# Attention and feed-forward kernel: fillers, one root and two unpacks reordered behind the loop, and six tiles' output base added on GpSimd inside it

## The chip, the cores and the metric

The kernel runs on one core of one Trainium2 chip. The metric is the device time in microseconds of one execution; the median of several runs is compared.

## The reference, cut to what matters

```python
x = x + L0_xattn(layernorm(x), tok, ctx, ctx, ctx)      # gated experts, one of four per token
x = x + L0_ffn(layernorm(x), w8)                        # fp8-quantised product
x = x + L1_xattn(layernorm(x), ctx, Wq, bq, Wkv, bkv, Wp, bp)
x = x + L1_ffn(layernorm(x), weight, bias)
```

x is (4, 256, 256) in f32, 1024 tokens of 256. Of the four steps two matter here:

```python
def L1_xattn(x, cond, ...):                 # 16 heads of 16, 1024 queries, 1024 keys
    q = fq_sym((x @ Wq + bq) * scale); k, v = fq_sym(cond @ Wkv + bkv)
    attn = fq_unsigned(softmax(q @ k.T))    # per head, rounded to 255 steps
    return (attn @ v) @ Wp + bp
def L1_ffn(x, weight, bias):
    return x @ ternary_quantize(weight).T + bias
```

## The kernel before, in words

The 1024 tokens lie in 8 tiles of 128 rows, sorted by expert. Each engine has its own program, written out by hand; semaphores tie them together. The first part (to about 118 us) makes keys, values, queries and the first two steps.

**The attention loop** runs over 8 tiles t and in each over 16 heads u. For one head TensorE makes the scores of 128 queries against 1024 keys (L1284) into one of three score buffers of two PSUM banks; VectorE takes the negative maximum of each row (`nmax`, L969); GpSimd makes the exponent's bias from it (`ebias`, `exp_bias`, L462); ScalarE makes the exponential, rounded to bytes (even heads) or 16-bit integers (odd heads) (L639). TensorE may write the scores of head u + 3 only when the exponential of head u is done. After every pair of heads SP's queue issues a transposing DMA (L362). What lands is in `rawT` (the trace calls its memory `ksplit`). The odd head is used from there; the even head's bytes must be unpacked to 16 bits into `byteT` (the trace says `gates`), by GpSimd in two casts of 128x512 (`unpack`, L473), which are called as the steps of the even and the odd head, 6 heads behind the bias. TensorE weighs the values with them 7 heads behind (`weigh`, L1313). To fill TensorE, `weigh` first issues four transposes that nobody reads (L1306), except where `fillers=False`.

In the same loop work of the tile before is put in: VectorE inverts the sums of the exponentials behind head 1 (L1001), divides behind head 9 (L1013), adds the projection to `xs` behind head 15 (`x3_ready`, L1007). GpSimd adds the projection's bias to `xs` in two halves, behind the casts at heads 9 and 10 (L484).

**Behind the loop** the work of the last tile and all of the fourth step remain. The tiles are in five units: (0, 1), (2, 3), (4, 5), (6), (7). For each unit: sums of the rows (`fourth_sums`, L1035 and L1039, VectorE), inverse root (`fourth_root`, L411 and L412, GpSimd; three roots, for tiles 0-1, 2-6 and 7), norm (`fourth_norm`, L932, VectorE), transposes (`h4_turn`, L1360, TensorE), copy (`copy_h4`, L665, ScalarE), products (`ternary`, L1371, TensorE), `output_base` (x + bias into `x4`, called `vq` in the trace; L1047, VectorE), `add_ternary` (L1052, VectorE), indirect store (`scatter_output`, L499, GpSimd, one per tile). In between the last tile's remaining heads 9 to 15 are weighed (`late_weigh`), divided, transposed (`att_turn`, L1321) and projected (`project`, L1329). Every engine takes its own list in order: GpSimd's is root 0, casts of heads 10 to 13, root 1, casts of 14 and 15, stores of units 0 and 1, root 2, stores of units 2 to 4.

## Time and profile before

| | us |
|---|---|
| three runs | 311.62, 311.80, 314.02 |
| median | 311.8 |
| the profiled execution | 311.21 |
| its span | 309.3 |
| busy in the span: VectorE / TensorE / ScalarE / GpSimd | 255.4 / 215.7 / 203.5 / 175.3 |

The profile is of one execution. Its rows give a start in microseconds from the start of the span, a busy time, the engine (PE is TensorE, PEld its weight load, DVE VectorE, ACT ScalarE, POOL GpSimd, SPq SP's queue), the line of the kernel, what is written from what, and how many instructions are merged into the row (x6). In square brackets stands idle time of the engine ahead of the row, and what ended it. Starts and ends of neighbours on VectorE overlap by some hundredths.

### The profile page before, as it was taken

Reading aid. Unit: us, or ns where it says so; the run is one execution under the profiler, and the core shown is the slowest. Engines: PE = TensorE matmul, PEld = TensorE weight load, DVE = VectorE, ACT = ScalarE, POOL = GpSimd, SP = SyncE. Lnnn points to the kernel's source line nnn. Section 1 sums busy time; section 2 is a strip of 40 time slices with the busy share of each in tenths; the row PEclk is TensorE's granted clock in tenths of the full one; section 3 lists DMA queues with packets and bytes.
Section 4 is the critical chain, followed back from the end, with each engine's and each line's share of the span. In section 5 each row is a group of like instructions: output and inputs, shape, how many; then the busy total and the mean of one; then the engine's idle time right before and its main releaser. Section 6 shows DMA issues by size and latency. Waiting matters only on the chain.

```text
span 309.3 us, 6042 instructions
## 1 busy us (share of the span) xinstructions
PE 215.7 (70%) x2042; PEld 149.0 (48%) x2072; DVE 255.4 (83%) x393; ACT 203.5 (66%) x352; POOL 175.3 (57%) x354
## 2 busy tenths in 40 slices
PE   4893189756526865587777787877877787776890
PEld 3441057544313751055555555555555555555670
DVE  2560969988869498979999999999999999999550
ACT  1100022544485736799999999999999999995020
POOL 2270242638742101377777767777777777786744
PEclk9999557999756795779999999999999999999787
DMA  7935000005999909979989899899989899899011
GB/s 248 305 110 153 1 1 2 0 0 95 178 197 178 170 0 180 177 146 168 149 172 165 161 155 155 155 159 147 175 160 158 162 169 150 160 155 156 17 52 68
DMA packets 133806, 41.03 MB, mean 133 GB/s; under 512 B 126352, under 2 KB 132880, under 8 KB 133776
## 3 DMA queue, kind: packets, MB, share of 16 engines
q1 hardware_dynamic: 131680, 37.24, 68.2%
q0 software_dynamic: 768, 2.10, 1.9%
q10 hardware_dynamic: 1328, 1.32, 1.3%
q8 instruction: 16, 0.26, 0.4%
q14 instruction: 14, 0.11, 0.1%
HBM read 5.25 MB, written 2.10 MB: 24 GB/s over the span
## 4 chain that ended last, share of the span: by engine, by line
ACT 24%; POOL 21%; DVE 18%; issue 16%; PE 12%; DMA 8%; POOLq 0%; ACTq 0%; DVEq 0%
ACT ctxT L639 11%; ACT ctx L639 11%; POOL gates L473 11%; POOL ebias L462 4%; DMA ksplit<-in_x 3%; PE ps L1155 3%; POOL scratch L406 2%; DMA xs<-scratch 2%; DMA ksplit<-ctxT 2%; POOL rstd L412 2%; DVE nmax L969 2%; PE ps L1284 1%; PE ps L1266 1%; POOL out L499 1%; DVE xs L862 1%
## 5 line engine op out<-in xcount | busy, mean ns | idle before, releaser
L969 DVE TENSOR_REDUCE nmax<-ps 128x1 f32<-128x1024 f32 x128 | 152.4, 1218 | 5.7 <-PE ps L1284 4.2
L1284 PE MATMUL ps<-keysT,kv 128*128 128x512 bf16 x226 | 74.3, 403 | 38.8 <-ACT ctx L639 22.3
L473 POOL CAST gates<-ksplit 128x512 int16<-128x512 uint8 x128 | 78.9, 618 | 10.2 <-DMA ksplit<-ctx 2.5
L639 ACT ACTIVATE ctx<-ps,ebias,qscale 128x1024 uint8<-128x1024 f32 x64 | 76.7, 1202 | 4.4 <-POOL ebias L462 4.4
L639 ACT ACTIVATE ctxT<-ps,ebias,qscale 128x1024 uint8<-128x1024 f32 x64 | 76.5, 1200 | 1.2 <-POOL ebias L462 1.2
L462 POOL TENSOR_SCALAR ebias<-nmax,qscale 128x1 f32<-128x1 f32 x128 | 33.9, 265 | 41.3 <-DVE nmax L969 38.0
L1306 PEld LDWEIGHTS ps<-identb 128*128 128x128 bf16 x400 | 30.9, 99 | 24.7 <-POOL gates L473 1.5
L1306 PE MATMUL ps<-identb 128*128 128x128 bf16 x400 | 39.2, 221 | 0.9 <-POOL gates L473 0.9
L1284 PEld LDWEIGHTS ps<-keysT,kv 128*128 128x128 bf16 x256 | 15.0, 98 | 49.5 <-ACT ctx L639 25.4
L532 ACT COPY hT<-ps 128x256 f32<-128x256 f32 x11 | 4.1, 371 | 46.0 <-PE ps L1147 46.0
L1313 PE MATMUL ps<-vals,gates 128*128 128x16 f16 x512 | 22.4, 170 | 0.4 <-POOL gates L473 0.4
L1313 PE MATMUL ps<-vals,ksplit 128*128 128x16 f16 x512 | 22.3, 170 | 0.1
L1313 PEld LDWEIGHTS ps<-vals,gates 128*128 128x128 f16 x512 | 20.4, 97 | 2.1 <-POOL gates L473 0.6
L1313 PEld LDWEIGHTS ps<-vals,ksplit 128*128 128x128 f16 x512 | 19.8, 96 | 1.2 <-ACT ctxT L639 0.2
L411 POOL TENSOR_SCALAR vareps<-mv 128x1 f32<-128x1 f32 (+4 forms) x14 | 3.7, 261 | 25.3 <-DVE mv L942 12.1
L1155 PE MATMUL ps<-ctxT,hT 128*128 (+1 forms) x44 | 14.8, 469 | 1.6 <-ACT hT L532 1.6
L406 POOL DMA_INDIRECT scratch<-ksplit,dest x8 | 8.5, 1056 | 11.9 <-DMA ksplit<-in_x 9.8
L1130 PE MATMUL ps<-wkv_s,ctxT 128*128 128x512 f32 x32 | 14.4, 598 | 0.7 <-ACT ctxT L526 0.7
L1155 PE MATMUL ps<-ctxT,gates 128*128 (+1 forms) x44 | 13.7, 441 | 0.3 <-ACT gates L538 0.3
L639 ACT ACTIVATION_READ_ACCUMULATOR ctxT<-ps,ebias,qscale 128x1 f32 x64 | 12.6, 196 | 0.0
L639 ACT ACTIVATION_READ_ACCUMULATOR ctx<-ps,ebias,qscale 128x1 f32 x64 | 12.4, 194 | 0.0
L1155 PEld LDWEIGHTS ps<-ctxT,hT 128*128 128x128 f32 x44 | 9.8, 236 | 4.4 <-issue 2.8
(187 smaller groups left out, 336.3 us busy)
## 6 DMA issues: line engine op xcount, KB each, us to landing
keysT<-zeros SPq DMA_DIRECT2D x4, 512.0 KB, 8.2
ctx<-in_ctx SPq DMA_DIRECT2D x2, 512.0 KB, 4.8
ksplit<-in_x ACTq DMA_DIRECT2D x1, 1024.0 KB, 10.8
xs<-scratch SPq DMA_DIRECT2D x1, 1024.0 KB, 5.6
wkv_s<-in_L_xattn_Wkv SPq DMA_DIRECT2D x1, 512.0 KB, 8.0
ksplit<-ctx SPq DMA_TRANSPOSE x32, 3.7
ksplit<-ctxT SPq DMA_TRANSPOSE x32, 3.8
bkv_b<-in_L_xattn_bkv ACTq DMA_DIRECT2D x1, 256.0 KB, 11.3
```

The lines of the kernel that those rows point to most:

```text
L406: g.indirect_dma_start(scratch, bass.IndirectOffsetOnAxis(ap=dest[:, t:t + 1], axis=0), record[:, t, :], None).then_inc(scattered, 16)
L412: root = g.tensor_tensor(rstd[:, lo:hi], vareps[:, lo:hi], half[:, 0:hi - lo], ALU.pow)
L462: g.tensor_scalar(ebias[:, slot], nmax[:, slot], qscale[:, t, u:u + 1], LN255, ALU.mult, ALU.add).then_inc(bias_ready, 1)
L473: g.tensor_copy(byteT[:, w % PT, part, :, :], rawT[:, w % PAIRS, part, :].bitcast(U8).rearrange("p b (q j) -> p b j q", j=2)).then_inc(unp ...
L532: a.copy(hT[:, j % 2, 0:C, :], ps[:, TRB[0], 0:D].rearrange("p (c q) -> p c q", c=C)).then_inc(hT_ready, 1)
L639: a.activation(probs, s_in, ACT.Exp, bias=ebias[:, u % 4:u % 4 + 1], scale=qscale[:, t, u:u + 1], accum_out=lsum[:, t, u:u + 1]).then_inc( ...
L969: v.tensor_reduce(nmax[:, u % 4:u % 4 + 1], score_banks(k, u), AX.X, ALU.max, negate=True).then_inc(max_ready, 1)
L1130: last = m.matmul(ps[:, KVB[r % 4], :], ctxT[:, c, r * P:(r + 1) * P], wkv_s[:, c, :], start=(c == 0), stop=(c == C - 1))
L1155: last = m.matmul(ps[:, bank, 0:D], lhs[:, c, :], ctxT_e[:, c, e, :], start=(c == 0), stop=(c == C - 1))
L1284: last = m.matmul(ps[:, bank + b, :], qT[:, t, u // 2, :], keysT[:, u % 2, u // 2, 512 * b:512 * b + 512], start=True, stop=True)
L1306: m.transpose(idle[:, i * P:(i + 1) * P], identb[:, :], identb[:, :])
L1313: last = m.matmul(out, probT.bitcast(F16), vals[:, r, u * HD:(u + 1) * HD], start=(r == 0), stop=(r == KT - 1))
```

## The change

- Loop, GpSimd: behind the casts at heads 4 and 5, from tile 2 on, half of tile t - 2 is added to the output bias into `x4`, after a wait for that tile's finished `xs` (`x3_ready`). That makes 12 additions of 128x128, for tiles 0 to 5.
- Behind the loop, VectorE: `output_base` 0, 1 and 2 go; a wait for the 12 additions (`based`) takes their place. Norm 3 moves ahead of addition 1, `output_base(3)` behind it, `output_base(4)` ahead of norm 4.
- GpSimd: root 1 moves ahead of the casts of heads 12 and 13 (the list is now root 0, casts 10 and 11, root 1, casts 12 and 13). The casts of heads 14 and 15 go.
- ScalarE: one copy of the same pair's 1024 columns (`unpack_last`), between the copies of turn 0 and turn 1; `weigh` of head 14 waits for it.
- TensorE: `late_weigh` issues its four unread transposes; `keep_warm` issues 10 more behind the loop, 4 behind turn 0 and 8 behind ternary 3; ternary 3 moves ahead of turn 4.

```diff
--- before.py
+++ after.py
@@ -49,6 +49,8 @@
 COPY_AT = 10
 PROJECT_AT = 11
 ADD_AT = 15
+BASE_AT = 4
+BASES = 6
 UNITS = ((0, 1), (2, 3), (4, 5), (6,), (7,))
 ROOTS = ((0, 2), (2, 7), (7, 8))
 
@@ -266,6 +268,7 @@
         linv_ready, att_ready, x3b_ready = sem("linv_ready"), sem("att_ready"), sem("x3b_ready")
 
         attT_full, attT_ready, proj_full, x3_ready = sem("attT_full"), sem("attT_ready"), sem("proj_full"), sem("x3_ready")
+        based, unpacked_last = sem("based"), sem("unpacked_last")
         h4T_full, h4T_ready, tern_full, x4_ready = sem("h4T_full"), sem("h4T_ready"), sem("tern_full"), sem("x4_ready")
 
 
@@ -482,6 +485,10 @@
                     if u in (BIAS_AT, BIAS_AT + 1):
                         part = slice((u - BIAS_AT) * P, (u - BIAS_AT + 1) * P)
                         g.tensor_tensor(xs[:, t, part], xs[:, t, part], bp_b[:, part], ALU.add).then_inc(x3b_ready, 1)
+                    if u in (BASE_AT, BASE_AT + 1) and t >= 2:
+                        pool.wait_ge(x3_ready, t - 1)
+                        part = slice((u - BASE_AT) * P, (u - BASE_AT + 1) * P)
+                        g.tensor_tensor(x4[:, t - 2, part], xs[:, t - 2, part], bt_b[:, part], ALU.add).then_inc(based, 1)
 
             pool.wait_ge(ld_b, 48)
             pool.wait_ge(h3_ready, NT)
@@ -500,10 +507,10 @@
                                          x4[:, t, :], None).then_inc(stored, 16)
 
             fourth_root(0)
-            for u in range(H - UNPACK_LAG, H - 2):
+            for u in range(H - UNPACK_LAG, H - 4):
                 unpack(NT - 1, u)
             fourth_root(1)
-            for u in range(H - 2, H):
+            for u in range(H - 4, H - 2):
                 unpack(NT - 1, u)
             pool.wait_ge(ld_order, 16)
             scatter_output(0)
@@ -665,7 +672,16 @@
                 a.copy(hT[:, i % 2, 0:n4, :].rearrange("p c q -> p (c q)"),
                        ps[:, TURN_BANKS[i], 0:n4 * P]).then_inc(h4T_ready, 1)
 
+            def unpack_last():
+
+                w = NP - 1
+                pair_turned(act, NT - 1, w)
+                act.wait_ge(pv_done, count(NT - 1, 2 * w - 2 * PT))
+                a.copy(byteT[:, w % PT, :, :, :],
+                       rawT[:, w % PAIRS, 0:KT // 2, :].bitcast(U8).rearrange("p b (q j) -> p b j q", j=2)).then_inc(unpacked_last, 1)
+
             copy_h4(0)
+            unpack_last()
             copy_h4(1)
             copy_att(NT - 1)
             for i in range(2, len(UNITS)):
@@ -1058,21 +1074,19 @@
             fourth_norm(0)
             invert_sums(last_tile)
             fourth_sums(4, 7)
-            output_base(0)
-            output_base(1)
             fourth_norm(1)
+            dve.wait_ge(based, 2 * BASES)
             add_ternary(0)
             divide(last_tile, last_tile)
             fourth_norm(2)
-            output_base(2)
+            fourth_norm(3)
             add_ternary(1)
-            fourth_norm(3)
+            output_base(3)
             add_projection(last_tile)
             dve.wait_ge(x3_ready, NT)
             fourth_sums(last_tile, NT)
-            output_base(3)
+            output_base(4)
             fourth_norm(4)
-            output_base(4)
             for i in range(2, len(UNITS)):
                 add_ternary(i)
 
@@ -1294,7 +1308,9 @@
 
             def weigh(t, k, u, fillers=True):
 
-                if u % 2 == 0:
+                if t == NT - 1 and u == H - 2:
+                    pe.wait_ge(unpacked_last, 1)
+                elif u % 2 == 0:
                     pe.wait_ge(unpacked, t * H + u + 2)
                 else:
                     pair_turned(pe, t, u // 2)
@@ -1382,11 +1398,18 @@
 
 
             def late_weigh(u):
-                weigh(NT - 1, NT - 1, u, fillers=False)
+                weigh(NT - 1, NT - 1, u)
+
+            def keep_warm(n):
+
+                for i in range(n):
+                    m.transpose(ps[:, TURN_BANKS[3], :].bitcast(BF16)[:, i % 8 * P:(i % 8 + 1) * P], identb[:, :], identb[:, :])
 
             pe.wait_ge(exp_done, NT * H)
+            keep_warm(10)
             late_weigh(9)
             h4_turn(0)
+            keep_warm(4)
             late_weigh(10)
             late_weigh(11)
             ternary(0)
@@ -1402,8 +1425,9 @@
             project(NT - 1, 1)
             ternary(2)
             h4_turn(3)
+            ternary(3)
+            keep_warm(8)
             h4_turn(4)
-            ternary(3)
             ternary(4)
```

## Rows read from the trace of the kernel before

**Rows 1.** Stretches, the attention loop: busy us and (x instructions) per engine; granted clock; DMA.

```profile
core 0: us, PE busy (x) PEld busy (x) DVE busy (x) ACT busy (x) POOL busy (x), PEclk, DMA share, GB/s
160.00:280.00 120.00, 93.72 (x1287) 67.67 (x1310) 117.52 (x115) 117.98 (x199) 88.76 (x205) 1.00 0.95 159
```

**Rows 2.** Timeline of VectorE, one tile of the loop.

```profile
243.27 9.63 DVE L969 TENSOR_REDUCE nmax<-ps 128x1 f32<-128x1024 f32 x8
252.82 0.41 DVE L1013 TENSOR_TENSOR krest<-ps,linv 128x256 f32<-128x256 f32 x1
...
263.29 9.63 DVE L969 TENSOR_REDUCE nmax<-ps 128x1 f32<-128x1024 f32 x8
```

**Rows 3.** Timeline of all engines, heads 3 to 13 of the last tile.

```profile
265.66 7.26 DVE L969 TENSOR_REDUCE nmax<-ps 128x1 f32<-128x1024 f32 x6
...
273.02 0.27 POOL L462 TENSOR_SCALAR ebias<-nmax,qscale 128x1 f32<-128x1 f32 x1 [0.30 <-DVE nmax L969]
...
273.32 1.20 ACT L639 ACTIVATE ctx<-ps,ebias,qscale 128x1024 int16<-128x1024 f32 x1
...
274.49 0.27 POOL L462 TENSOR_SCALAR ebias<-nmax,qscale 128x1 f32<-128x1 f32 x1
...
274.67 0.60 PE L1284 MATMUL ps<-keysT,kv 128*128 128x512 bf16 x2 [0.23 <-ACT ctx L639]
...
275.39 0.45 POOL L484 TENSOR_TENSOR xs<-xs,bp_b 128x128 f32<-128x128 f32 x1
...
275.93 0.27 POOL L462 TENSOR_SCALAR ebias<-nmax,qscale 128x1 f32<-128x1 f32 x1
```

**Rows 4.** Timeline behind the loop, VectorE and GpSimd.

```profile
283.23 0.73 DVE L932 TENSOR_SCALAR hs<-xs,mv,rstd 128x256 f32<-128x256 f32 x2 [0.26 <-POOL rstd L412]
...
285.09 0.32 DVE L1039 BATCH_NORM_AGGREGATE mv<-stats 128x2 f32<-128x6 f32 x3
...
285.27 2.20 POOL L473 CAST gates<-ksplit 128x512 int16<-128x512 uint8 x2 [0.25 <-DMA ksplit<-ctxT]
...
287.77 1.20 POOL L412 TENSOR_TENSOR rstd<-vareps,half 128x5 f32<-128x5 f32 x1
...
288.93 1.23 POOL L473 CAST gates<-ksplit 128x512 int16<-128x512 uint8 x2
...
289.08 1.23 DVE L932 TENSOR_SCALAR hs<-xs,mv,rstd 128x256 f32<-128x256 f32 x2 [2.08 <-POOL rstd L412]
```

**Rows 5.** Stretches behind the loop: columns as in rows 1.

```profile
282.30:285.70 3.40, 1.66 (x30) 1.31 (x30) 3.07 (x14) 0.63 (x2) 2.41 (x5) 1.00 0.78 174
285.70:289.00 3.30, 3.30 (x11) 2.40 (x11) 1.26 (x2) 0.00 (x0) 3.22 (x5) 0.50 0.09 20
289.10:292.40 3.30, 2.14 (x39) 1.89 (x36) 2.69 (x6) 0.59 (x1) 1.71 (x3) 1.00 0.00 0
```

**Rows 6.** Timeline of TensorE, last fillers of the loop, and ternary 0 to 2.

```profile
280.28 0.38 PE L1306 MATMUL ps<-identb 128*128 128x128 bf16 x4
280.50 0.35 PE L1313 MATMUL ps<-vals,ksplit 128*128 128x16 f16 x8
...
285.49 3.61 PE L1371 MATMUL ps<-wtT,hT 128*128 128x256 f32 x8
...
291.69 3.04 PE L1371 MATMUL ps<-wtT,hT 128*128 128x256 f32 x8 [0.29 <-ACT hT L665]
...
296.72 1.95 PE L1371 MATMUL ps<-wtT,hT 128*128 128x256 f32 x8
```

**Rows 7.** Timeline near the end: a turn's copy, stores, last statistics.

```profile
291.05 0.59 ACT L665 COPY hT<-ps 128x512 f32<-128x512 f32 x1 [5.75 <-PE ps L1360]
...
297.06 0.96 POOL L499 DMA_INDIRECT out<-vq,token_of  x1 [0.31 <-issue]
...
297.84 0.18 DVE L1039 BATCH_NORM_AGGREGATE mv<-stats 128x2 f32<-128x6 f32 x1
...
299.52 0.42 DVE L1047 TENSOR_TENSOR vq<-xs,bt_b 128x256 f32<-128x256 f32 x1
...
304.88 0.96 POOL L499 DMA_INDIRECT out<-vq,token_of  x1 [0.30 <-issue]
```

## The prediction, with its working

> **What bounds the kernel now.** I read the stretches first [rows 1]: over 120 us of the attention loop VectorE is busy 117.52 us, ScalarE 117.98, GpSimd 88.76. GpSimd's spare quarter looks like room for more work. But occupancy doesn't say whether a delay there is harmless, so next I read the loop head by head.
>
> VectorE's timeline [rows 2] shows one tile: eight maxima from 243.27 without a gap (9.63 us), the division at head 9, and the same eight maxima of the next tile from 263.29, 20.02 us later. Time that VectorE loses here is lost for good.
>
> The timeline of all engines [rows 3] shows what each maximum hangs on. Six maxima end at 265.66 + 7.26 = 272.92; at one 1.22 us long that is a start every (7.26 - 1.22) / 5 = 1.21. The bias on GpSimd starts at 273.02 (0.10 later), ScalarE's exponential at 273.32 (0.30 later), and the scores that reuse the buffer of the exponential before it are made after that. From the start of the exponential at 273.32 to the end of the scores that it releases, at 274.67 + 0.60 = 275.27, it is 1.95. With three score buffers a round is 1.22 + 0.10 + 0.30 + 1.95 = 3.57 us and a signal; three maxima take 3.62. So the ring has at most 0.05 us of slack: a bias that comes late makes a later maximum late.
>
> Behind the loop [rows 4 to 7] there is a chain: roots, norms, turns, ternary products, the projection of the last tile, its root and norm, then four stores that GpSimd issues one after the other.
>
> **Part 1: the base of six tiles in the loop.** Removed behind the loop are `output_base` 0, 1 and 2; added are two additions of 128x128 in each of tiles 2 to 7, twelve in all, on GpSimd right behind the casts of heads 4 and 5. The same form exists at heads 9 and 10 [rows 3]: 0.45 us. There two biases stand 275.93 - 274.49 = 1.44 apart instead of 1.21. So one addition makes the next bias 0.23 late and two in a row 0.46. With a cast alone GpSimd can repeat after about 1.44 - 0.45 = 1.0 us, so it is level again some three heads later.
>
> ScalarE isn't: an exponential is busy for 1.20 against the 1.21 of the maxima, so it wins back a hundredth per head. Heads 5 and 6 start 0.23 and 0.46 late, head 7 stays 0.46 late behind head 6. Less 0.04 of slack, the maxima of heads 8 and 9 start about 0.2 and 0.43 late in all, and nothing behind them is shorter. At heads 9 and 10 the old additions do little, because VectorE's division (0.41, [rows 2]) puts the next maximum off by more than the bias is late; heads 4 and 5 have no such cover. The wait on `x3_ready` costs nothing: what it asks for is done at head 15 of the tile before. The loop pays **6 x 0.43 = 2.6 us**. Bounds: nothing, if the ring has half a microsecond of slack that I don't see, and the full occupation of GpSimd, (0.45 + 0.09) x 12 = 6.5, 0.09 being the gap from the addition's end (275.84) to the bias. I take 2.6, as it comes from rows of the same form in the same loop.
>
> **Part 2: root 1 ahead of two unpacks, last pair to ScalarE.** Before [rows 4], GpSimd casts heads 12 and 13 for 2.20 us (to 287.47), then makes the root of tiles 2 to 6 (power from 287.77, 1.20) and casts 14 and 15. Now the root only waits for the sums that end at 285.09 + 0.32 = 285.41: 0.40 for the signal and the small addition, power to 287.0, norm 1 from 287.1 to about 288.35, casts 12 and 13 from 287.0 to 288.24, priced as the two at 288.93 (1.23). They cost less than 2.20 because no `output_base` runs beside them. Late next are heads 12 and 13: their casts end 0.77 later than before. The casts of 14 and 15 become one copy of 1024 on ScalarE. There is no row of this form; bounds are 0.59, the copy of 512 columns from PSUM [rows 7], and 2.5, twice what GpSimd takes for the same two casts. I take 1.2, the exponential of the same width [rows 3]. The transfers have ended by about 286.0 (a share of 0.09 of the 3.3 us from 285.7, [rows 5]), so the copy is over by 288.5 at worst, and head 14 comes to TensorE at 289.5. The copy of turn 1, queued behind it on ScalarE, is needed at 289.8. Cost nothing; cover 1.0 us.
>
> Norm 1 meets casts 12 and 13 now, as it met casts 14 and 15 before; there it took 1.23 against 0.73 for the like norm 0 [rows 4]. The Trainium skill (SBUF — State Buffer, "SBUF: two separate sides") says that such a VectorE operation and a GpSimd one lock a shared pair of ports for a whole instruction, whichever starts first. The rows agree as far as one of the two grew. By that rule the norm could win and the casts end up to 0.5 later, and the gain below would shrink by 0.5.
>
> **Part 3: TensorE, fillers and clock.** Four unread transposes put the next products off by 280.50 - 280.28 = 0.22 us [rows 6]. `keep_warm(10)` takes some 0.55 and lies in the idle behind the loop, in which head 9 is filled too; `keep_warm(4)` lies in the wait for head 10's casts. Heads 10 to 15 each pay 0.22. Ternary 0 starts 0.44 later, at 285.93.
>
> The granted clock [rows 5]: 1.00 up to 285.7, while TensorE was busy 1.66 of 3.40 us; then 0.50 (1.2 GHz) to 289; then 1.00, with 2.14 of 3.30 busy; behind that, ternary 1 again ran slowly. Ternary 0 and 1 took 3.61 and 3.04 us, ternary 2 took 1.95 [rows 6]. The fillers raise 1.66 to about 2.5 of 3.40, and the waits in the middle shrink, so I take the high level throughout. What it gives is what the rows at either level differ by.
>
> Ternary 0: 285.93 to 287.9, off the path, since the casts of 12 and 13 are only there at 288.24. Heads 12 and 13 at 0.43 each until 289.10, turn 1, its copy (0.59, [rows 7]) 289.8 to 290.4, heads 14 and 15 until 290.4, ternary 1 **290.48 to 292.43**; before, 291.69 to 294.73. That is 2.30 us earlier, 1.21 of it from the earlier start and 1.09 from the clock.
>
> **Part 4: the end.** Before, the last root, about 298.1, had two predecessors almost level: the first four stores on GpSimd (297.06 + 0.96 = 298.02) and the last tile's statistics (297.84 + 0.18 = 298.02) [rows 7]. The stores follow ternary 1 by 298.02 - 294.73 = 3.29; now they end at 292.43 + 3.29 = 295.72. The projection follows ternary 1 by less than before, as its products run at the high clock, and is no longer the later one. `output_base(3)` is covered by VectorE's wait for the projection, `output_base(4)` by the wait for the root; it stood at 299.52 in front of addition 2, with 0.42 and a gap: 0.43 saved. So 2.30 from ternary 1 and 0.43 from the order: together **2.7 us**. Bounds for the tail: 0.4 (start and clock give nothing) and 3.2. Ternary 3 and 4 have cover: the last store at 304.88 waits for nothing but GpSimd itself ("issue").
>
> **Sum.** 311.21 (profiled execution: span 309.3 and 1.9 around it) + 2.6 - 2.7 = 311.1. The profiled execution lies 0.6 under the median of the runs, 311.8, so **311.7 us**.
>
> **Rivals.**
> Low clock in part of the tail. For it: the clock fell after 2.14 of 3.30 busy, no large gap. Against: hardly an idle stretch over 0.6 us is left. If ternary 0 takes 3.61, it ends 289.54, turn 1 follows at 290.40, 1.30 later: gain 1.4, time 311.8 + 2.6 - 1.4 = 313.0; if ternary 1 takes 3.04, the gain is 1.6 and the time 312.8; if both, or if the fillers do nothing for the clock and only cost their 0.22s, 0.4 is left: 314.0.
>
> The additions are hidden: the maxima don't feel half a microsecond of a late bias. For it: GpSimd is idle for a quarter of the loop. Against: ScalarE has no idle to give. Time 311.8 - 2.7 = 309.1.
>
> Slower: each addition holds VectorE up by GpSimd's full 0.54, because the lag of heads 4 and 5 meets the additions at 9 and 10 before it is gone. 12 x 0.54 - 2.7 = 3.8: 315.6. It turns the change slower by over 1% from (3.1 + 2.7) / 12 = 0.48 per addition on. Against it: three heads between at 1.0 against 1.21.
>
> **Chances.** Forecast 0.50 (311.0 to 312.4), low clock 0.22 (312.5 to 314.1), hidden 0.15 (about 309), slower 0.07 (315 and more), anything else 0.06. The range reaches from the hidden case to one or two low stretches: 309.0 to 313.6. A measurement can tell about 1% (3.1 us) from no change. Faster by over 1% needs the hidden case and a better tail: 0.08; slower by over 1%: 0.12; within: 0.80.
>
> **What will show it.** VectorE's timeline of a tile from 2 on: idle of about 0.2 us twice, at heads 8 and 9, and a tile of 20.45 instead of 20.02. Behind the loop: the power of root 1 0.4 behind the sums; a granted clock of 1.00 from the loop's end on; ternary 1 near 1.95 us; the last root right behind the stores of unit 1, not behind the statistics. The forecast is wrong if a tile stays at 20.0 or grows by a microsecond, or if the clock shows 0.50 before the last products.

## The result, and the profile after

| | before | changed |
|---|---|---|
| median of 22 runs | 311.67 us | 313.75 us |
| ratio changed / before | | 1.0054, 95% interval 1.0034 to 1.0074 |
| span of the profiled execution | 309.3 | 312.0 |

The change costs about 1.7 us by the ratio (1.1 to 2.3). The forecast was no change, 311.7, with a range of 309.0 to 313.6. The sign of each part was as forecast, a loss in the loop and a gain behind it, but the loss was larger and the gain much smaller.

VectorE's timeline cuts each profile into three parts: up to the start of the first maximum, from there to the end of the last maximum, and from there to the end of the span.

| profile | first part | loop | behind it |
|---|---|---|---|
| before, the one the forecast used | 118.8 | 161.8 | 28.65 |
| changed | 120.5 | 164.9 | 26.55 |

The first part has no edit in it; the next section comes back to it. The loop lost 3.1, the rest gained 2.1.

A fourth share lies outside the span. An execution of the changed kernel takes 2.13 to 2.23 us more than its span in all 22 runs. The kernel before takes 1.80 to 1.96 more in the 29 runs timed beside e1. So about 0.3 of the 1.7 us is not in the profile at all, and the forecast took the 1.9 us as fixed. It belongs neither to the additions alone (1.76 in e2) nor to the rest of the change alone (1.75 in e1). What makes it stays open.

**The loop.** The stretch that answers to [rows 1] (same columns; VectorE, the third pair, was at 117.52):

```profile
160.00:280.00 120.00, 91.89 (x1260) 66.09 (x1282) 115.10 (x112) 115.97 (x194) 91.32 (x211) 1.00 0.92 156
```

VectorE lost 2.4 us of work in 120, GpSimd rose from 88.76 to 91.32. VectorE's timeline of one tile, for [rows 2]:

```profile
185.49 7.21 DVE L985 TENSOR_REDUCE nmax<-ps 128x1 f32<-128x1024 f32 x6
192.92 1.22 DVE L985 TENSOR_REDUCE nmax<-ps 128x1 f32<-128x1024 f32 x1 [0.22 <-PE ps L1298]
194.37 1.23 DVE L985 TENSOR_REDUCE nmax<-ps 128x1 f32<-128x1024 f32 x1 [0.22 <-PE ps L1298]
195.51 0.41 DVE L1029 TENSOR_TENSOR krest<-ps,linv 128x256 f32<-128x256 f32 x1
...
205.98 1.16 DVE L985 TENSOR_REDUCE nmax<-ps 128x1 f32<-128x1024 f32 x1
```

The eight maxima of heads 2 to 9 are no longer in one piece: ahead of heads 8 and 9 VectorE waits 0.22 us each for scores. The tile takes 205.98 - 185.49 = 20.49 us instead of 20.02.

One such wait was there before, in the part of the tile that [rows 2] leaves out, ahead of head 14's maximum:

```profile
258.21 2.41 DVE L969 TENSOR_REDUCE nmax<-ps 128x1 f32<-128x1024 f32 x2 [0.23 <-PE ps L1284]
```

It stands four to five heads behind the old additions at heads 9 and 10, and in every tile. So "at heads 9 and 10 the old additions do little" looks like a misreading: the kernel before already paid 0.23 us per tile behind them. ScalarE's copy of the attention (0.36) falls in the same place, and no run takes either out, so it isn't shown which of them makes the wait. The same tile on GpSimd and ScalarE, for [rows 3]:

```profile
190.08 0.46 POOL L491 TENSOR_TENSOR vq<-xs,bt_b 128x128 f32<-128x128 f32 x1
...
190.63 0.26 POOL L465 TENSOR_SCALAR ebias<-nmax,qscale 128x1 f32<-128x1 f32 x1
...
191.53 0.45 POOL L491 TENSOR_TENSOR vq<-xs,bt_b 128x128 f32<-128x128 f32 x1
...
192.07 0.26 POOL L465 TENSOR_SCALAR ebias<-nmax,qscale 128x1 f32<-128x1 f32 x1
...
190.93 1.20 ACT L646 ACTIVATE ctxT<-ps,ebias,qscale 128x1024 int16<-128x1024 f32 x1 [0.15 <-POOL ebias L465]
...
192.37 1.20 ACT L646 ACTIVATE ctxT<-ps,ebias,qscale 128x1024 uint8<-128x1024 f32 x1 [0.15 <-POOL ebias L465]
```

Two biases stand 192.07 - 190.63 = 1.44 us apart, as at the old additions, and ScalarE, which waited for nothing there before, waits 0.15 for a bias twice.

**Behind the loop**, first GpSimd, VectorE and ScalarE, for [rows 4]; the last maximum ends at 285.45 here and at 280.65 before:

```profile
290.63 1.20 POOL L415 TENSOR_TENSOR rstd<-vareps,half 128x5 f32<-128x5 f32 x1
...
291.79 1.23 POOL L476 CAST gates<-ksplit 128x512 int16<-128x512 uint8 x2
...
291.86 1.30 DVE L948 TENSOR_SCALAR hs<-xs,mv,rstd 128x256 f32<-128x256 f32 x2 [1.66 <-POOL rstd L415]
...
291.34 1.05 ACT L680 CAST gates<-ksplit 128x1024 int16<-128x1024 uint8 x1 [1.24 <-DMA ksplit<-ctxT]
```

The power of root 1 starts 5.2 us behind the last maximum instead of 7.1. Norm 1 takes 1.30, beside the casts. The copy on ScalarE takes 1.05.

Then TensorE, VectorE and GpSimd, for [rows 6] and [rows 7]:

```profile
290.71 1.97 PE L1387 MATMUL ps<-wtT,hT 128*128 128x256 f32 x8
...
295.05 0.35 PE L1329 MATMUL ps<-vals,ksplit 128*128 128x16 f16 x8
295.26 1.98 PE L1387 MATMUL ps<-wtT,hT 128*128 128x256 f32 x8
...
296.73 0.42 DVE L1029 TENSOR_TENSOR krest<-ps,linv 128x256 f32<-128x256 f32 x1 [2.97 <-PE ps L1329]
297.07 1.05 DVE L948 TENSOR_SCALAR hs<-xs,mv,rstd 128x256 f32<-128x256 f32 x3
298.04 0.68 DVE L1068 TENSOR_TENSOR vq<-ps,vq 128x512 f32<-128x512 f32 x1
...
299.00 0.96 POOL L506 DMA_INDIRECT out<-vq,token_of  x1 [1.97 <-DVE vq L1068]
...
301.26 0.26 POOL L414 TENSOR_SCALAR vareps<-mv 128x1 f32<-128x1 f32 x1
...
307.60 0.96 POOL L506 DMA_INDIRECT out<-vq,token_of  x1 [0.30 <-issue]
```

Ternary 0 and 1 take 1.97 and 1.98 us. The stretches that hold them show the granted clock (columns as in [rows 1]; the third number from the end is the clock, 1.00 for 2.4 GHz and 0.50 for 1.2 GHz):

```profile
290.00:293.00 3.00, 2.68 (x32) 2.13 (x30) 1.34 (x5) 1.15 (x2) 2.62 (x4) 1.00 0.30 68
293.00:297.00 4.00, 3.93 (x60) 3.60 (x60) 1.03 (x3) 0.59 (x1) 2.11 (x3) 1.00 0.09 33
```

Both ran at the full clock. Ternary 1 starts 295.26 - 285.45 = 9.8 us behind the last maximum; before it was 11.0. But addition 1 doesn't follow it at once: it stands behind the division and norms 2 and 3, and the division starts only at 296.73, after 2.97 us of idle, although head 15's products are over at 295.40 by their rows (the rows of TensorE give starts; their ends are modelled). The chain of work that ended last (start, us, what) names the link:

```profile
294.98 0.24 PE ps L1322 x4
295.22 1.42 PE ps L1329 x8
296.64 0.03 issue
296.66 0.02 DVEq L1028
296.69 0.04 issue
296.73 0.42 DVE krest L1029
```

Head 15's products stand in it with 1.42 us: that is the time to their signal, the semaphore that the division waits for. It is new; in the kernel before the division started 0.45 us behind the start of these products (291.06 to 291.51).

### The profile page after: what moved, and what is told of

It is laid out like the page before. It is cut to its first block, busy times and chain, and to the rows that moved or that the text cites. A ratio compares the mean times of both kernels' runs of the same rounds, so it can differ in the third digit from the quotient of the medians.

```text
span 312.0 us, 6147 instructions
## 1 busy us (share of the span) xinstructions
PE 220.5 (71%) x2092; PEld 151.4 (49%) x2122; DVE 253.1 (81%) x390; ACT 205.7 (66%) x353; POOL 177.8 (57%) x364
## 4 chain that ended last, share of the span: by engine, by line
POOL 31%; issue 20%; DVE 17%; PE 12%; ACT 12%; DMA 6%; POOLq 0%; ACTq 0%; DVEq 0%
POOL gates L476 16%; POOL ebias L465 6%; ACT ctxT L646 5%; ACT ctx L646 5%; PE ps L1169 4%; DMA ksplit<-in_x 4%; POOL rstd L415 2%; POOL scratch L409 2%; POOL out L506 2%; PE ps L1298 2%; DMA xs<-scratch 2%; DVE nmax L985 1%; PE ps L1280 1%; PE ps L1329 1%; DMA scratch<-ksplit,dest 1%
## 5 line engine op out<-in xcount | busy, mean ns | idle before, releaser
L1298 PE MATMUL ps<-keysT,kv 128*128 128x512 bf16 x226 | 75.7, 410 | 40.7 <-ACT ctx L646 22.2
L476 POOL CAST gates<-ksplit 128x512 int16<-128x512 uint8 x126 | 76.7, 610 | 9.2 <-DMA ksplit<-ctx 1.6
L1322 PEld LDWEIGHTS ps<-identb 128*128 128x128 bf16 x428 | 32.8, 99 | 26.0 <-POOL gates L476 2.6
L1322 PE MATMUL ps<-identb 128*128 128x128 bf16 x428 | 42.0, 221 | 1.4 <-POOL gates L476 1.3
L414 POOL TENSOR_SCALAR vareps<-mv 128x1 f32<-128x1 f32 (+4 forms) x14 | 3.6, 258 | 27.4 <-DVE mv L958 12.1
L1144 PE MATMUL ps<-wkv_s,ctxT 128*128 128x512 f32 x32 | 16.2, 663 | 0.7 <-ACT ctxT L533 0.7
L409 POOL DMA_INDIRECT scratch<-ksplit,dest x8 | 8.2, 1024 | 12.0 <-DMA ksplit<-in_x 9.9
```

Source lines behind the costliest of these rows:

```text
L409: g.indirect_dma_start(scratch, bass.IndirectOffsetOnAxis(ap=dest[:, t:t + 1], axis=0), record[:, t, :], None).then_inc(scattered, 16)
L476: g.tensor_copy(byteT[:, w % PT, part, :, :], rawT[:, w % PAIRS, part, :].bitcast(U8).rearrange("p b (q j) -> p b j q", j=2)).then_inc(unp ...
L1144: last = m.matmul(ps[:, KVB[r % 4], :], ctxT[:, c, r * P:(r + 1) * P], wkv_s[:, c, :], start=(c == 0), stop=(c == C - 1))
L1298: last = m.matmul(ps[:, bank + b, :], qT[:, t, u // 2, :], keysT[:, u % 2, u // 2, 512 * b:512 * b + 512], start=True, stop=True)
L1322: m.transpose(idle[:, i * P:(i + 1) * P], identb[:, :], identb[:, :])
```

## Was the one profile of before typical?

The first two experiments to read are two further profiles of the kernel before, unchanged.

> The kernel before, once more, for a second profile. The loss that loop and tail don't explain (about 0.7 us of 1.7) is put down to the one profile that the sum was made against. Theory: the first part (first maximum at 118.8 us) and the part behind the loop (28.65 us from the last maximum's end, with two stretches at the low clock) vary from profile to profile; another profile of the same kernel has its first maximum at 120 or later, or another number of slow ternary products, while its tiles still take 20.03 us. Rival: the changed kernel has a longer first part; then this one shows 118.8 again.

> The kernel before, a third profile, for the same question: first maximum between 118.5 and 121, from the last maximum's end to the end of the span between 26.9 (no slow product) and 28.7 us (two slow ones), tiles of 20.03 us.

Measured, with other profiles for comparison (us; tile: the usual length among tiles 2 to 6; "division" is its start behind the start of head 15's products; in e12 VectorE is busy with output base until then). The other runs are told in the sections that follow.

| profile | first part | tile | loop | behind it | ternary 0 / 1 | division |
|---|---|---|---|---|---|---|
| before | 118.8 | 20.03 | 161.8 | 28.65 | 3.61 / 3.04 | 0.45 |
| before, again (e5) | 120.4 | 20.03 | 162.1 | 27.53 | 3.78 / 1.99 | 0.45 |
| before, third (e6) | 120.2 | 20.03 | 161.9 | 27.32 | 3.66 / 1.99 | 0.45 |
| changed | 120.5 | 20.49 | 164.9 | 26.55 | 1.97 / 1.98 | 1.68 |
| changed, again (e4) | 120.7 | 20.50 | 165.5 | 26.58 | 1.97 / 1.98 | 1.65 |
| e1, base on VectorE | 120.3 | 20.05 | 162.0 | 27.23 | 1.97 / 1.98 | 1.68 |
| e2, additions alone | 120.9 | 20.52 | 165.1 | 27.76 | 3.78 / 1.99 | 0.45 |
| e10, covered slots | 119.1 | 20.20 | 163.1 | 26.62 | 1.97 / 1.98 | 1.67 |
| e11, no fillers | 119.8 | 20.49 | 164.8 | 26.53 | 3.78 / 1.99 | 0.45 |
| e12, best | 121.8 | 20.04 | 162.4 | 25.89 | 1.97 / 1.98 | 1.23 |

TensorE's ternary products 0 and 1 in e5, for [rows 6]:

```profile
287.73 3.78 PE L1371 MATMUL ps<-wtT,hT 128*128 128x256 f32 x8
...
293.61 1.99 PE L1371 MATMUL ps<-wtT,hT 128*128 128x256 f32 x8 [0.29 <-ACT hT L665]
```

and in e6:

```profile
286.90 3.66 PE L1371 MATMUL ps<-wtT,hT 128*128 128x256 f32 x8
...
292.94 1.99 PE L1371 MATMUL ps<-wtT,hT 128*128 128x256 f32 x8 [0.29 <-ACT hT L665]
```

The granted clock agrees, in the forecast's profile for ternary 1 and in e5 for ternary 0 and ternary 1:

```profile
293.00:295.00 2.00, 2.00 (x8) 1.52 (x7) 0.34 (x2) 0.00 (x0) 0.98 (x1) 0.50 0.33 119
...
289.00:291.00 2.00, 2.00 (x6) 1.53 (x6) 0.01 (x1) 0.00 (x0) 1.92 (x4) 0.50 0.00 0
...
293.00:295.00 2.00, 1.71 (x19) 1.47 (x17) 1.57 (x4) 0.56 (x1) 1.14 (x1) 1.00 0.00 0
```

Ternary 0 is slow in all three profiles of before, ternary 1 in one of three. That one was the forecast's. So 1.1 us of the 28.65 were not a fixed property of the kernel. In the two other profiles the length is about 27.4, and the changed kernel gains 0.9 on it, not 2.1. How often ternary 1 is slow can't be told from three profiles; their average is 27.8. The first part goes from 118.8 to 121.8 in this table with no edit in it, and the unchanged kernel has 120.4 and 120.2 in e5 and e6: the 1.7 us by which the changed kernel's first part is longer are not the change's.

The changed kernel again:

> The changed kernel, once more, for a second profile. Tiles of 20.49 us and a division 1.3 us behind head 15 are properties of the program and come back; the start of the first maximum (120.5 us against 118.8 in the kernel before) differs from profile to profile if it depends on TensorE's clock in the first part, and stays at 120.5 if the change has lengthened it.

Tiles of 20.50, division 1.65 behind the start of head 15's products, 26.58 behind the loop; ratio to before 1.0067 (1.0038 to 1.0095). What the change does is the same in both profiles; the first part, 120.7, doesn't tell the two theories apart, but e5 and e6 do.

## The loop's price: experiments with the additions

**e1: without the additions.**

```diff
-                    if u in (BASE_AT, BASE_AT + 1) and t >= 2:
...
             fourth_sums(4, 7)
+            output_base(0)
+            output_base(1)
             fourth_norm(1)
-            dve.wait_ge(based, 2 * BASES)
             add_ternary(0)
+            output_base(2)
             divide(last_tile, last_tile)
```

> The changed kernel with its twelve additions in the loop taken out again; output base 0 and 1 are made by VectorE while it waits for root 1, output base 2 ahead of the division. Everything else behind the loop as changed. Ring theory (the additions in the loop cost 6 x 0.46 = 2.8 us plus what the last tiles show, the part behind the loop saves 2.1): tiles of 20.03 us, from the last maximum's end to the end of the span 26.6 us as in the changed kernel, time 2.8 to 3.1 under the changed kernel and 2.1 under the kernel before (ratio to before about 0.993). Rival, the additions are free and the loss lies in the first part or in the tail: ratio to before 1.003 to 1.007 as the changed kernel has.

Ratio to before 0.9961 (0.9927 to 0.9996). The loop is back at 162.0 with tiles of 20.05. Against the changed kernel, timed beside it (1.0067), that is 1% or 3.3 us less. Behind the loop it is 27.23 us, 0.6 more than expected, which is most of the distance from 0.993 to 0.996; the interval holds both. The rows of VectorE and GpSimd show where that is:

```profile
287.04 1.39 DVE L1059 TENSOR_TENSOR vq<-xs,bt_b 128x512 f32<-128x512 f32 x2
...
287.88 1.60 POOL L415 TENSOR_TENSOR rstd<-vareps,half 128x5 f32<-128x5 f32 x1
```

Output base 0 and 1 run beside root 1, and the power takes 1.60 instead of 1.20; the small addition ahead of it 0.58 instead of 0.25. Counted from the last maximum, norm 1 and the casts come 0.8 later than in the changed kernel. The two additions on VectorE, 1.39, hardly suffer (two alone take 1.41 in e12). The Trainium skill (SBUF — State Buffer, "SBUF: two separate sides") says that a VectorE operation with two SBUF inputs and a GpSimd operation that reads SBUF take the shared pair of ports one at a time; the trace agrees with it in this place, the loser being GpSimd.

**e2: the additions alone**, on the kernel before.

```diff
+                    if u in (BASE_AT, BASE_AT + 1) and t >= 2:
...
-            output_base(0)
-            output_base(1)
             fourth_norm(1)
+            dve.wait_ge(based, 2 * BASES)
...
-            output_base(2)
```

> The kernel before with only the twelve additions on GpSimd in the loop and output base 0 to 2 taken out behind it. Ring theory: tiles 2 to 7 take 20.49 instead of 20.03 us, with VectorE idle 0.22 us ahead of the maxima of heads 8 and 9; loop +2.8 to 3.1; behind the loop the casts of heads 12 and 13 lose the company of output base and take 1.2 instead of 2.2, worth up to 0.8; together +2.0 to +3.0 (ratio 1.006 to 1.010). Rival, the additions are hidden: ratio 0.998 to 1.000.

Ratio 1.0052 (1.0019 to 1.0085), loop 165.1, tiles of 20.52 us; behind the loop 27.76, so the up to 0.8 that taking output base off VectorE was to bring there didn't come. The casts of heads 12 and 13 did take 1.18 instead of 2.20, but ternary 0, at 3.78, stands in front of these heads on TensorE anyway. At +1.6 (0.6 to 2.7) the time is under the +2.0 to +3.0 expected, though the interval reaches into it. The parts of its one profile add to more: 3.1 in the loop and 0.3 behind it, against the 27.4 of e5 and e6. A longer usual tail of the kernel before would close some of this; no run settles it. By the ratio the additions alone carry as much loss as the whole change.

**e10: the same additions where VectorE has work of its own.**

```diff
-BASE_AT = 4
+BASE_SLOTS = (1, 15)
...
-                    if u in (BASE_AT, BASE_AT + 1) and t >= 2:
+                    if u in BASE_SLOTS and t >= 2:
```

> The changed kernel with the two additions per tile behind the casts of heads 1 and 15 instead of 4 and 5, where VectorE puts in work of its own (the inversion, 0.16 us net, behind head 1's maximum; the addition of the projection, 0.33 net, behind head 15's). An addition makes the next bias 0.23 late; VectorE's own work puts that bias off by 0.16 and 0.33 anyway, so at most 0.07 per tile is left. Ring theory: tiles 2 to 7 take 20.03 to 20.10 us instead of 20.50, time 2.4 to 2.8 under the changed kernel, ratio to before 0.996 to 0.999. Rival (the cost is GpSimd's occupation, wherever it stands): 20.5 again.

Ratio 1.0003 (0.9973 to 1.0033). VectorE's timeline of one tile:

```profile
223.96 3.60 DVE L985 TENSOR_REDUCE nmax<-ps 128x1 f32<-128x1024 f32 x3
227.73 6.03 DVE L985 TENSOR_REDUCE nmax<-ps 128x1 f32<-128x1024 f32 x5 [0.17 <-PE ps L1298]
...
244.15 3.60 DVE L985 TENSOR_REDUCE nmax<-ps 128x1 f32<-128x1024 f32 x3
```

The tile takes 244.15 - 223.96 = 20.19. One new wait is left, 0.17 ahead of head 5's maximum: by the three buffers it comes from the bias of head 2, so of the 0.23 by which the addition behind head 1 delays the next bias, the inversion covers little. Behind head 15 nothing is left. So the price of an addition isn't GpSimd's 0.54: it is 0.23 where it is bare, and 0 to 0.17 where VectorE's own work puts the next maximum off. The expected 0.07 was too small by 0.1, as it counted the inversion's 0.16 as slack of the whole ring. The ratio missed its 0.996 to 0.999 too: six tiles cost 1.0, and the 0.3 outside the span is there as well (2.13 to 2.29 in its ten runs).

## Behind the loop: clock, fillers and a late signal

**e11 and e13: without the added transposes**, first one profile, then timed.

```diff
             def late_weigh(u):
-                weigh(NT - 1, NT - 1, u)
+                weigh(NT - 1, NT - 1, u, fillers=False)
-            keep_warm(10)
...
-            keep_warm(4)
...
-            keep_warm(8)
```

> The changed kernel without any of the added unread transposes. Tiles of 20.50 as changed. Clock theory: ternary 0 takes 3.6 to 3.8 us at the low clock as in all three profiles of the kernel before, ternary 1 about 2.0 in most profiles; the division starts 0.45 behind head 15; from the last maximum's end to the span's end 27.0 to 27.8 instead of 26.6. Rival (the fillers give nothing, order alone brought the gain): 26.6 or less, with 3.6 for ternary 0.

> The changed kernel without the added transposes, timed. Its one profile had ternary 0 at 3.78 us (low clock), ternary 1 at 1.99, and 26.53 us behind the loop, against 26.55 with fillers. Theory (clock and fillers cancel: what the clock gives, the fillers' own time and the late division take back): time within 0.3% of the changed kernel, ratio to before 1.003 to 1.008. Rival (the fillers save a slow ternary 1 in a good part of the executions, worth 1.1 us each): up to 0.5 us slower than the changed kernel.

Ratio to before 1.0056 (1.0037 to 1.0076), that of the changed kernel. Behind the loop 26.53 and 26.51 us, against 26.55 with fillers. TensorE's products and the division of e11:

```profile
289.73 3.78 PE L1387 MATMUL ps<-wtT,hT 128*128 128x256 f32 x8
...
295.09 1.99 PE L1387 MATMUL ps<-wtT,hT 128*128 128x256 f32 x8 [0.29 <-ACT hT L672]
...
294.91 0.43 DVE L1029 TENSOR_TENSOR krest<-ps,linv 128x256 f32<-128x256 f32 x1 [0.59 <-PE ps L1329]
```

Ternary 0 takes 3.78 and ternary 1 starts 0.7 us later than with fillers (10.5 behind the last maximum against 9.8). But the division comes 0.45 behind head 15, and addition 1 starts 12.56 behind the last maximum, with fillers 12.59. The fillers do hold the clock, and in this kernel they give nothing: what ternary 0 and head 15 win, the late division gives back. So e11's expected 27.0 to 27.8 was wrong and its rival right. The 0.9 us of the tail are the order's: root 1 ahead of the casts, the last pair on ScalarE, and output base off the end, taken together; no run separates the three.

**Why the division is late** is the question of e3, e7, e8, e9, e15 and e16, all on the changed kernel, with one profile each. "Behind" means behind the start of head 15's products.

> The changed kernel with four more unread transposes between head 15 of the last tile and ternary product 1. In the changed kernel the division started 1.33 us behind the modelled end of head 15's products (1.42 us for the eight by the chain), while ternary 1 followed them at once. Theory of the late signal: the f32 products right behind head 15's hold its signal up; with transposes between, the division starts about 0.1 us behind head 15, addition 1 is bound by ternary 1 again and the end comes about 0.4 us earlier (0.6 less the 0.2 of the fillers). Rival: the division waits for something else; it starts 1.3 us behind head 15 as before, and the time is 0.2 us longer or the same. The time difference is too small to measure; the division's start in the trace decides.

```diff
             late_weigh(15)
+            keep_warm(4)
             ternary(1)
```

Division 1.67 behind: f32 products right behind head 15 are not the cause; 26.62 us behind the loop. That theory fell.

> The changed kernel; TensorE waits for the signal of its own head 15 before it starts ternary 1. Theory of the pause: in the kernel before and in the one with the additions alone TensorE paused 0.29 us behind head 15 and the division started 0.45 us behind the start of head 15's products; without a pause it started 1.65 to 1.68 us behind. With a forced pause it should be 0.45 again, ternary 1 starts 0.1 to 0.2 later, addition 1 and the end come 0.4 to 0.6 us earlier. Rival (fillers ahead of the products hold the signal up): it stays at 1.65 and ternary 1 starts 1.3 us later.

```diff
             late_weigh(15)
+            pe.wait_ge(pv_done, NT * H)
             ternary(1)
```

Head 15's products, ternary 1 and the division:

```profile
293.98 0.35 PE L1329 MATMUL ps<-vals,ksplit 128*128 128x16 f16 x8
...
295.62 1.99 PE L1387 MATMUL ps<-wtT,hT 128*128 128x256 f32 x8 [1.29 <-PE ps L1329]
...
295.67 0.42 DVE L1029 TENSOR_TENSOR krest<-ps,linv 128x256 f32<-128x256 f32 x1 [2.98 <-PE ps L1329]
```

TensorE itself waits for the signal and gets it as late as VectorE: the division stays 1.69 behind, ternary 1 starts 1.4 us later, 27.22 behind the loop. The theory of the pause fell too. The signal itself is late against the rows, whoever reads it.

> The changed kernel; the fillers of heads 14 and 15 stand behind head 15 instead of ahead of each, so TensorE makes no pause. Theory of the pause: the division still starts some 1.2 us or more behind the end of head 15's products. Rival (fillers ahead hold the signal up): 0.1 us behind, and the end comes earlier.

```diff
-            late_weigh(14)
-            late_weigh(15)
+            weigh(NT - 1, NT - 1, 14, fillers=False)
+            weigh(NT - 1, NT - 1, 15, fillers=False)
+            keep_warm(8)
             ternary(1)
```

Division 0.65 behind, no pause of TensorE, ternary 1 at the full clock, 25.99 behind the loop: 0.56 under the changed kernel, with the same number of transposes. The theory of the pause had 1.2 or more here; its rival is the nearer one.

> The changed kernel; of heads 14 and 15 only head 15 has its four transposes ahead, head 14's stand behind head 15. Division 1.65 us behind the start of head 15's products if transposes right ahead of a head hold up its own signal; 0.65 if it takes those of head 14.

> The changed kernel; only head 14 has its four transposes ahead, head 15's stand behind it. Division 0.45 to 0.65 us behind the start of head 15's products if only transposes right ahead of a head hold up its own signal; 1.2 or more if what counts is how much TensorE was given before without a pause.

These are e8 with four of the eight back ahead of head 15 or of head 14. Both give 1.17 behind (26.02 and 26.03 behind the loop), which neither value of e15's expectation had. So it isn't the place right ahead of the head: eight transposes ahead of the two heads give 1.65 to 1.69, four 1.17, none 0.65, and none anywhere behind the loop 0.45. From 0.65 on each of them costs 0.13 us of signal, on top of the 0.055 that it takes in TensorE's rows (0.22 for four).

> The changed kernel; the four unread transposes ahead of each of heads 9 to 15 of the last tile go to a bank that the heads' products don't use (in the changed kernel they go to the second half of the bank that the products accumulate in). With the fillers ahead of heads 14 and 15 the division started 1.65 to 1.69 us behind the start of head 15's products, with them behind 0.65, without them 0.45. Theory of the bank: now it is 0.45 to 0.65, the part behind the loop takes 26.0 us instead of 26.6. Rival: any transposes right ahead do it, 1.65 again and 26.6.

```diff
             def late_weigh(u):
-                weigh(NT - 1, NT - 1, u)
+                keep_warm(4)
+                weigh(NT - 1, NT - 1, u, fillers=False)
```

Division 1.16 behind, between the two expectations, 25.85 behind the loop. That looks as if the bank had half a part, but the edit changes a second thing. `weigh` waits for the head's casts and then issues its transposes; the new call issues them ahead of the wait. TensorE's rows at head 12 show it, first the changed kernel, then e9:

```profile
293.07 0.40 PE L1322 MATMUL ps<-identb 128*128 128x128 bf16 x4 [0.39 <-POOL gates L476]
...
292.27 0.36 PE L1329 MATMUL ps<-vals,gates 128*128 128x16 f16 x8 [0.26 <-POOL gates L476]
```

This is TensorE's last pause ahead of head 15. Between it and head 15 the changed kernel, e3, e4 and e7 issue 16 transposes (heads 12 to 15), e9, e15 and e16 issue 12, and e8 issues 8. The division comes 1.65 to 1.69, 1.16 to 1.17 and 0.65 behind. So the count since the last pause covers all of these runs, and the bank needs no part. It is near the second alternative of e16's expectation, but the count was put to the rows afterwards, and no run tests the bank or the pause alone. That head 12's transposes moved into the pause also explains why ternary 1 starts 0.2 earlier in e9 (9.6 behind the last maximum), and with it part of the 25.85.

What delays the signal is not settled. One open rival is that the transposes take TensorE longer than the 0.055 of their rows, so that what follows runs later than its own rows say; e7 would look the same. The signal of a large product can be late too: in e8, with eight transposes right ahead of ternary 1, addition 1 starts 2.23 us behind the start of ternary 1, against 2.03 to 2.04 in e7, e11 and e14. Against a plain lag stands turn 1 of the changed kernel, behind the transposes of heads 12 and 13: it ends at 294.57 and ScalarE copies at 294.61.

## A version that beats both

**e12**: no additions in the loop; output base on VectorE in idle time that lies beside neither root 1 nor the casts; fillers of heads 14 and 15 behind them (as e8).

```diff
             fourth_sums(4, 7)
             fourth_norm(1)
-            dve.wait_ge(based, 2 * BASES)
+            output_base(0)
             add_ternary(0)
+            output_base(1)
+            output_base(2)
             divide(last_tile, last_tile)
```

> No additions in the loop; output base 0 behind norm 1, output base 1 and 2 ahead of the division, all on VectorE in its idle time and beside neither root 1 nor the casts; fillers of heads 14 and 15 behind them; all else as changed. Expected: tiles of 20.03, 26.0 us behind the loop against 27.3 to 27.5 in two of the three profiles of the kernel before: 1.4 under the kernel before, ratio 0.994 to 0.997. If output base costs there what it saves in the loop, 0.998 to 1.000.

Ratio to before 0.9955 (0.9925 to 0.9986). VectorE's timeline behind root 1:

```profile
290.63 1.30 DVE L944 TENSOR_SCALAR hs<-xs,mv,rstd 128x256 f32<-128x256 f32 x2 [1.66 <-POOL rstd L415]
291.85 0.68 DVE L1059 TENSOR_TENSOR vq<-xs,bt_b 128x512 f32<-128x512 f32 x1
292.56 0.69 DVE L1064 TENSOR_TENSOR vq<-ps,vq 128x512 f32<-128x512 f32 x1
293.17 1.41 DVE L1059 TENSOR_TENSOR vq<-xs,bt_b 128x512 f32<-128x512 f32 x2
294.61 0.42 DVE L1025 TENSOR_TENSOR krest<-ps,linv 128x256 f32<-128x256 f32 x1
```

Output base 0, 1 and 2 all fit between norm 1 and the division, which starts when they end. 25.89 us behind the loop, tiles of 20.04, as expected. The time outside the span is 1.69 to 1.78 us in its twelve runs.

**e14**: the same without any added transposes.

> No additions in the loop, output base on VectorE in its idle time, root 1 ahead, last pair by ScalarE, and no added transposes. If the fillers are worth nothing: 26.0 to 26.6 us behind the loop and the ratio of the best kernel with fillers (0.9955) to within its interval; if they are worth 0.5 us or more there: 0.997 to 0.999.

Ratio 0.9964 (0.9935 to 0.9992), 26.76 behind the loop. The profiles differ by 0.9, and the timed runs can't tell the two apart. The 26.76 lies above the 26.0 to 26.6 expected for fillers without worth, the ratio at their side. So what the fillers are worth in this version stays open. The heading holds for both versions: each interval lies below 1, while that of the changed kernel lies above it.

## Why the prediction was wrong, step by step

- **The ring of three buffers, right.** Place (heads 8 and 9), size of the wait (about 0.2 twice) and tile (20.45 forecast, 20.49 measured) are those of part 1. Its 6 x 0.43 = 2.6 was 6 x 0.46 = 2.8, as the 0.04 us of slack didn't show. The whole loop grew by 3.2: 165.2 on the average of the two profiles of the changed kernel, 162.0 on that of the three of before. The rest are stalls in single tiles, as 0.5 in tile 1 of e4, where nothing is added. The rival "hidden" fell with e2, the rival of 0.54 per addition with the 0.23 of every tile. Its sentence on the old additions at heads 9 and 10 left out a wait of VectorE of 0.23 us per tile behind them.
- **Part 2, right.** Root 1 directly behind the sums (power 0.43 behind them), casts 1.23 beside norm 1, which took 1.30; ScalarE's copy 1.05 (1.2 forecast), off the path. The "up to 0.5" by which the casts could end later didn't come.
- **Part 3, the mechanism right, its worth wrong.** Ternary 1 from 9.8 to 11.8 behind the last maximum is what the sum had. But 1.09 of the 2.30 were "from the clock", and in two of three profiles of the kernel before ternary 1 has the full clock anyway (1.99 us in e5 and e6). This step failed: one profile's low clock was taken for the kernel's, and the gain was measured against 28.65 us behind the loop where two of three profiles have 27.4.
- **Part 4, a wait that the forecast didn't have, 0.6 to 0.7 us.** This step failed too. The stores were to follow ternary 1 by 3.29; they ended 301.22 - 297.24 = 3.98 behind it, since addition 1 waited for the division and norms 2 and 3. The forecast kept the 3.29 of before and so took the division and the norms to be done by then, which the 0.45 us of the kernel without fillers would have allowed. The division came 1.23 later than that, and the new order of VectorE's list (norm 3 ahead of addition 1) put one more instruction of 0.4 between the division and addition 1. The last root did stand right behind the stores, as forecast.
- **Sum.** Forecast -0.1. The tail of before was 0.8 (average of three) to 1.2 (two of three) shorter than assumed, the late division cost 0.6, the loop 0.6 more, and the time outside the span grew by 0.3. That gives +2.2 to +2.6, at or above the upper end of the measured 1.1 to 2.3. What gives the difference back is open; the first part, which varies by 2 us and more from execution to execution, is in the timed runs and not in this sum.
- **The range.** It ended at 313.6, and the changed kernel's median is 313.75. That this lies in the bracket of the low-clock rival (312.5 to 314.1) is luck: the clock stayed high in both profiles of the changed kernel until its last products. The range did count a low clock in the changed kernel, but not that the kernel before could lack it.
- **The rival in which the fillers only cost** was half right. Their worth in the changed kernel is nothing (e11, e13), though they hold the clock. The gain of only 0.4 that it left for the tail was too low, as the order alone brings 0.9.

## What to carry to other kernels

Before work is given to an engine because its occupancy is low, follow one round of the buffers through all engines: here GpSimd had a quarter of its time free and no slack that could be seen, and each addition of 0.45 us cost the loop 0.23. Read the timeline of the bounding engine over a whole tile: the wait of 0.23 us behind the old additions of the same form was there before the change. Put such work where the bounding engine does something of its own, and then look at the ring again. A term that rests on TensorE's clock in one profile needs a second profile of the same kernel. Compare also the time outside the span, which no row shows. And with transposes put in as fillers, look at when the signals of the products behind them arrive, not only at when the products end.

## What the hardware showed that I had not expected

- A signal of TensorE can come 1.2 us behind the end that its rows model. From the start of head 15's eight products to VectorE's start it was 0.45 us without added transposes, 0.65 with 8 of them since TensorE's last pause, 1.16 to 1.17 with 12 and 1.65 to 1.69 with 16. TensorE waiting for its own signal (e7) sees the same. Whether the signal or the rows are off isn't settled.
- VectorE's additions with two SBUF inputs slowed GpSimd's power from 1.20 to 1.60 us and the small addition ahead of it from 0.25 to 0.58 (e1). Beside norm 1 the casts kept their 1.23 and the norm grew from 0.73 to 1.30. In the loop, where VectorE reads PSUM, GpSimd's addition took 0.45 as always.
- Ternary 0 at the full clock (1.97) instead of the low one (3.78) brought ternary 1 forward by 0.7 us and the end by nothing, as the division came late (changed against e11). With the fillers behind the heads it went with 1.0 us at ternary 1 and 0.9 behind the loop (e12 against e14, one profile each), which the timed runs don't confirm.
- The time outside the span was 2.13 us or more in every run of the changed kernel and at most 2.00 in every run of the kernel before timed beside the experiments.
